# Reordering the first pass of an adaLN + ternary-FFN kernel: attended values next to scores, out products one unit later, ternary compares in halves

## What is computed

```python
# x (32, 32, 256), cond (32, 256); 16 heads of 128
ada = cond @ ada_w + ada_b                       # shift1, scale1, gate1, shift2, scale2, gate2
x1 = _ln(x) * (1.0 + scale1) + shift1
q, k, v = x1 @ qkv_w + qkv_b                     # reshaped (32, 32, 3, 16, 128)
attn = softmax(einsum('bthd,bshd->bhts', q, k) * scale)
x = x + gate1 * (einsum('bhts,bshd->bthd', attn, v) @ out_w + out_b)
x2 = _ln(x) * (1.0 + scale2) + shift2
x = x + gate2 * (gelu(x2 @ ffn_w1 + ffn_b1) @ ffn_w2 + ffn_b2)
# then x + bitffn(x): three linear layers whose weights are made ternary,
# wq = round(tanh(w / mean|w|)) * arctanh(mean|w|), and whose inputs are quantised to 8 bits
```

## Time and profile before

| what | value |
|---|---|
| median of three runs | 317.27 us (315.52, 317.27, 318.60) |
| profiled execution, its own time | 314.79 us |
| its span in the profile | 313.0 us |
| between the two | 1.79 us |
| TensorE busy, share of the span | 305.9 us, 98% |
| granted TensorE clock, mean | 1.00 |

### The profile page before, as it was taken

One profiled execution on the slowest core, in us unless ns is written; L12 is line 12 of the kernel. 1 busy time (PEld: TensorE's weight loads), 2 busy tenths in 40 slices (PEclk: granted clock), 3 DMA queues, 4 the chain that ended last, 5 costly groups with the idle time before them and its releaser, 6 DMA issues.

```text
span 313.0 us, 9827 instructions
## 1 busy us (share of the span) xinstructions
PE 305.9 (98%) x4171; PEld 271.4 (87%) x4171; DVE 223.7 (71%) x451; ACT 185.7 (59%) x358; POOL 128.0 (41%) x109
## 2 busy tenths in 40 slices
PE   8999999999999999999999999999999999999986
PEld 6888989899898989989898998789997789998664
DVE  3675889847795994634569057879277888996996
ACT  2765474645534664466344936587655677468793
POOL 2366406200930992766120621147330255323590
PEclk9999999999999999999999999999999999999999
DMA  7789944500044546210020010200010200200011
GB/s 234 268 227 274 290 148 181 168 4 2 2 116 89 162 114 235 69 36 2 3 70 2 2 35 3 63 7 2 20 50 2 69 4 2 69 0 2 0 36 68
DMA packets 21171, 24.49 MB, mean 78 GB/s; under 512 B 2020, under 2 KB 18696, under 8 KB 21128
## 3 DMA queue, kind: packets, MB, share of 16 engines
q1 hardware_dynamic: 20752, 23.57, 25.0%
q10 hardware_dynamic: 376, 0.30, 0.3%
HBM read 22.74 MB, written 1.11 MB: 76 GB/s over the span
## 4 chain that ended last, share of the span: by engine, by line
PE 93%; DVE 2%; ACT 2%; issue 1%; ACTq 0%; DVEq 0%
PE proj_banks L589 43%; PE out_bank L589 16%; PE wide_banks L589 5%; PE turn_bank L589 5%; PE proj_banks L654 4%; PE att_banks L685 4%; PE wide_banks L884 2%; PE att_banks L589 2%; PE wide_banks L685 2%; PE att_banks L931 2%; PE att_banks L918 1%; ACT work L1977 1%; PE wide_banks L768 1%; PE att_banks L884 1%; PE proj_banks L884 1%
## 5 line engine op out<-in xcount | busy, mean ns | idle before, releaser
L1834 ACT ACTIVATE q_t<-proj_banks,bias_cols 128x256 f32<-128x256 f32 x64 | 30.4, 475 | 48.6 <-PE proj_banks L589 47.8
L589 PE MATMUL proj_banks<-x_hi,w_hi 128*128 128x256 f32 x252 | 52.5, 290 | 0.0
L589 PE MATMUL proj_banks<-x_hi,w_lo 128*128 128x256 f32 x252 | 49.6, 278 | 0.0
L589 PE MATMUL proj_banks<-x_lo,w_hi 128*128 128x256 f32 x252 | 49.6, 278 | 0.0
L589 PEld LDWEIGHTS proj_banks<-x_hi,w_hi 128*128 128x128 f32 x252 | 38.6, 188 | 3.6 <-issue 1.6
L589 PEld LDWEIGHTS proj_banks<-x_hi,w_lo 128*128 128x128 f32 x252 | 38.3, 188 | 0.0
L589 PEld LDWEIGHTS proj_banks<-x_lo,w_hi 128*128 128x128 f32 x252 | 38.2, 188 | 0.0
L1305 DVE TENSOR_TENSOR v_sb<-proj_banks,bv_row 128x512 f32<-128x512 f32 x32 | 22.0, 687 | 17.1 <-PE proj_banks L589 15.9
L1834 ACT ACTIVATE k_t<-proj_banks,bias_cols 128x256 f32<-128x256 f32 x64 | 30.1, 470 | 0.0
L1839 ACT ACTIVATE scores<-scores 128x256 f32<-128x256 f32 x16 | 6.7, 418 | 32.2 <-DVE scores L1314 32.2
L1337 DVE STREAM_TRANSPOSE att_banks<-att_banks 128x512 f32<-128x512 f32 x16 | 11.6, 727 | 18.4 <-PE wide_banks L685 17.9
(11 more groups left out here) (329 smaller groups left out, 790.5 us busy)
## 6 DMA issues: line engine op xcount, KB each, us to landing
stage<-in_L_cond_qkv_w SPq DMA_DIRECT2D x16, 256.0 KB, 3.6
gate<-gate_rows_scratch SPq DMA_DIRECT2D x48, 64.0 KB, 2.5
stage<-in_L_cond_qkv_w SPq DMA_DIRECT2D x4, 512.0 KB, 5.1
stage<-in_L_cond_out_w SPq DMA_DIRECT2D x16, 128.0 KB, 4.3
work<-in_L_ffn_w SPq DMA_DIRECT2D x2, 1024.0 KB, 5.6
xin<-in_x SPq DMA_DIRECT2D x7, 256.0 KB, 2.9
bv_row<-in_L_cond_qkv_b SPq DMA_DIRECT2D x4, 256.0 KB, 6.4
work<-in_L_cond_ada_w SPq DMA_DIRECT2D x1, 1024.0 KB, 8.7
```

Source lines behind the costliest of these rows:

```text
L589: mm = pe.matmul(dst, l, r, start=start and i == 0, stop=stop and i == len(seq) - 1)
L1834: act.activation(dst[:, h, :], proj_bank[h % 2][:, s * QT:(s + 1) * QT], ACT.Identity, bias=bias_cols[:, c:c + 1]).then_inc(qk_kept, 1)
```

## The change

1. In units 2 to 7 (`V_LAST`) TensorE runs head 0, 1, 2, 3, then attend(u - 1), score(u), v 0, v 1. To make room, heads, scores and value rows swap the halves of `proj_banks` from unit to unit (`head_bank`, `packed(u)`, `v_bank`). The second value unit now waits for `shifted` (the scores have been read), score(u) no longer for a value row.
2. Out products of u - 1 move into unit u + 1, behind its head 1 (those of 0 stay in unit 1).
3. `tern_turn` moves to units 5, 7 and 9; each pair of compares is split (`tern_below`, `tern_make`) over two units. The third pair is now in unit 8, its transposes follow score(9), and its two copies (`tern_keep(2, 0)` and `(2, 1)`) stand on ScalarE ahead of heads 0 and 1 of unit 10.
4. On VectorE `softmax_shift(u)` moves between the two `at_turn`; on ScalarE `exponent(u)` between the two `at_high`, and `acc_keep` ahead of head 2 of units 3, 5 and 7.
5. On SyncE the wait for `tern_turned` at 6 and the load of g3 move behind later loads. `split_qk(2, 0)` on VectorE moves ahead of the tail of unit 6.

```diff
-    TERN_UNITS = (3, 5, 6)
+    TERN_UNITS = (5, 7, HALF + 1)
+    V_LAST = range(2, HALF)
...
-        packed = proj_bank[0][:, 0:2 * HG * TB]
+        def head_bank(u, h):
+            return proj_bank[(h + u) % 2 if u in V_LAST else h % 2]
+        def packed(u):
+            return head_bank(u, 0)[:, 0:2 * HG * TB]
+        def v_bank(u, t):
+            return head_bank(u, 1 - t if u in V_LAST else t)
...
             sp.dma_start(f2_stage, ffn2_d).then_inc(f2_in, 16)
-            sp.wait_ge(tern_turned, 2 * len(TERN_ORDER))
-            sp.dma_start(g3_row[:, :], row(g3)).then_inc(g3_in, 16)
             sp.wait_ge(v_kept, 2 * HALF)
             load_bv(3)
             wo_split(2)
             load_wo(3)
             sp.wait_ge(gate1_read, 4)
             load_gate(gate1, 0, 0, gate1_in)
+            sp.wait_ge(tern_turned, 2 * len(TERN_ORDER))
+            sp.dma_start(g3_row[:, :], row(g3)).then_inc(g3_in, 16)
...
+                elif h == 0 and u - 1 in V_LAST:
+                    pe.wait_ge(v_kept, 2 * u - 1)
...
-                pe.wait_ge(qk_kept, 2 * HG * u + 2 * HG - 2 + 2 * t)
+                if u in V_LAST and t == 1:
+                    pe.wait_ge(shifted, u + 1)
+                else:
+                    pe.wait_ge(qk_kept, 2 * HG * (u + 1) - (0 if u in V_LAST else 2 - 2 * t))
...
-                elif u in TERN_UNITS:
-                    pe.wait_ge(tern_kept, 2 * TERN_UNITS.index(u) + 2)
+                elif u + 1 in TERN_UNITS[:2]:
+                    pe.wait_ge(tern_kept, 2 * TERN_UNITS.index(u + 1) + 2)
+                elif u == TERN_UNITS[2]:
+                    pe.wait_ge(tern_kept, 2 * len(TERN_UNITS))
...
+                if u in TERN_UNITS:
+                    tern_turn(TERN_UNITS.index(u))
+                if u > 2:
+                    for t in range(2):
+                        out_proj(u - 2, t)
                 qk_unit(u, 2)
-                if u > 1:
+                qk_unit(u, HG - 1)
+                if u in V_LAST:
                     attend(u - 1)
-                qk_unit(u, HG - 1)
+                    score(u)
...
                 v_unit(u, 0)
                 v_unit(u, 1)
                 score(u)
+                if u in TERN_UNITS:
+                    tern_turn(TERN_UNITS.index(u))
                 out_proj(u - 1, 0)
...
             def attention_tail(u):
+                at_turn(u - 1, 0)
+                if u in V_LAST:
+                    softmax_shift(u)
+                at_turn(u - 1, 1)
+                keep_v(u, 0)
+                at_low(u - 1, 0)
+                if u in V_LAST:
+                    keep_v(u, 1)
+                at_low(u - 1, 1)
...
             softmax_norm(HALF - 1)
+            below = tern_below(2, n)
...
+                if q == 0:
+                    tern_make(2, below)
...
                 for h in ((1, 0, 2, 3) if u == 1 else range(HG)):
-                    if u - 1 in TERN_UNITS and h < 2:
-                        tern_keep(TERN_UNITS.index(u - 1), h)
+                    if h == 2 and u in TERN_UNITS:
+                        for b in range(2):
+                            tern_keep(TERN_UNITS.index(u), b)
+                    if h == 2 and u > 2 and u % 2 == 1:
+                        acc_keep(u // 2 - 1)
                     keep_qk(u, h)
...
                 for h in range(HG):
+                    if u - 1 == TERN_UNITS[2] and h < 2:
+                        tern_keep(2, h)
                     keep_qk(u, h)
```

More of the change, by code:

```diff
@@ L647, in score @@
                 pe.wait_ge(qk_kept, 2 * HG * (u + 1))
-                pe.wait_ge(v_kept, 2 * u + 1)
+                if u not in V_LAST:
+                    pe.wait_ge(v_kept, 2 * u + 1)
                 for t in range(2):
@@ L653, in score @@
                             tok = slice(t * P + j * TB, t * P + (j + 1) * TB)
-                            mm = pe.matmul(packed[j * TB:(j + 1) * TB, cols], q_t[:, h, tok], k_t[:, h, tok],
+                            mm = pe.matmul(packed(u)[j * TB:(j + 1) * TB, cols], q_t[:, h, tok], k_t[:, h, tok],
                                            start=True, stop=True)
@@ L762, in tern_turn @@
                     pe.wait_ge(tern_kept, 2 * p)
-                pe.wait_ge(at_lo_made, 2 * TERN_UNITS[p])
+                pe.wait_ge(at_lo_made, 2 * TERN_UNITS[p] - (2 if TERN_UNITS[p] in V_LAST else 0))
                 for b in range(2):
@@ L1282, in tern_make @@
                     dve.wait_ge(tern_turned, 2 * (p - 1))
-                n = own.up(dve.tensor_scalar(dst, tern_stage[i], thr[:, i, 1:2], None, ALU.is_lt))
+                return own.up(dve.tensor_scalar(dst, tern_stage[i], thr[:, i, 1:2], None, ALU.is_lt))
+            def tern_make(p, n):
+                i, dst = TERN_ORDER[p], tern[p % 2]
                 after(n)
@@ L1603, in _ @@
                         late_conditions()
+                    else:
+                        tern_make(0, below)
                     x1_make(u // 2 + 1)
@@ L1606, in _ @@
                     x_norm(3)
-                    tern_make(0, tern_thresholds(0))
+                    below = tern_below(0, tern_thresholds(0))
                 elif u == 5:
-                    tern_make(1, tern_thresholds(1))
+                    below = tern_below(1, tern_thresholds(1))
                 elif u == 6:
-                    tern_make(2, n)
+                    tern_make(1, below)
+                    split_qk(2, 0)
                 elif u == 7:
@@ L1615, in _ @@
                     split_qk(3, 0)
-                attention_tail(u)
+                if u > 0:
+                    attention_tail(u)
                 if u == 5:
@@ L2009, in _ @@
                 if u > 0:
-                    for t in range(2):
-                        at_high(u - 1, t)
+                    at_high(u - 1, 0)
+                    if u in V_LAST:
+                        exponent(u)
+                    at_high(u - 1, 1)
                 if u == 0:
@@ L2029, in _ @@
                     load_table(ACT.Exp)
[L2030 to L2035, removed]
             for q in range(NQ):
```

39 lines of the change are left out of this document (18 added, 21 removed).

## The result

| | before | changed |
|---|---|---|
| median, the two run by turns (22 executions each) | 315.44 us | 318.07 us |
| ratio of the times, 95% interval | | 1.0065 [1.0043, 1.0088] |
| profiled execution: span | 313.0 us | 316.1 us |
| mean granted clock in it | 1.00 | 0.995 |

A forecast was written before the change was run, and what follows sets the result against it. TensorE's issue of matmuls was taken as the bound. First pass -1.2 + 0.2 + 0.4 = -0.6 us, plus 2.6 us waiting for g3, made +2.0 on 317.27: 319.3 us, 0.6% slower, range 316.2 to 322.2.

The forecast's parts named there:

- Edit 1: Units 2 to 7: attend and score side by side remove 0.20 us of tile-shape losses in each, -1.2 us.
- Wait (a): Score(u) on TensorE, 1.00 us behind head 3, needs ScalarE's copy of it; 0.03 a unit, 0.2 us in all.
- Wait (b): Value unit 1 on TensorE waits for VectorE's shift of the scores; slack 0.4 us, nothing charged.
- rival C: Units 4 to 7: at_turn on VectorE over 0.4 us late, delaying value unit 1; 2 us more, chance 0.12.
- Edit 2: Out products moved later, between two runs of 256 columns on TensorE: no shape change or wait, nothing charged.
- Edit 3: Ternary transposes in units 5 and 7, between head 1 and out products: loss on both sides, 0.4 us.
- The row of gains: Attend(9) in unit 10 waits for ScalarE's work queued behind the later load of g3; 2.6 us.
- L: Time the load of g3 takes to land after SyncE issues it; taken as 4.4 us, ends 3.4 and 7.7.
- L - 1.8: TensorE's wait before attend(9): the landing time of g3 less 1.8 us; 2.6 us, ends 1.6 and 5.9.
- the estimate of 4.8: Landing of g3 by a fixed 2 us plus growth with bytes: 4.8 us, making attend(9)'s wait 3.0 us.
- Rival D: The clock falls in the new wait before attend(9), slowing it and two heads; up to 3.9 us more, chance 0.04.

The follow-up runs named there:

- shape_between: copies_first with one full-array matmul of 128 columns, its result unread, between attend and score in units 6 and 7; one execution, 313.84 us.
- copies_first: The changed kernel with both ternary copies of unit 10 ahead of the scaling of g3 on ScalarE; 314.27 us, ratio to before 0.9972.
- scale_late: The changed kernel with only the scaling of g3 moved behind exponent(10) on ScalarE; 314.91 us, ratio to before 0.9997.
- row_twice: The changed kernel with g3 loaded twice, one load behind the other, ScalarE waiting for both; 322.72 us, ratio to before 1.0231.
- scale_between: The changed kernel with the scaling of g3 between head 0's copy and the second ternary copy on ScalarE; 315.20 us, ratio to before 1.0013.

## Why the prediction was right

The sign, the place and the size held, +2.05 us against +2.0; the absolute time was 1.2 us too high: the kernel before took 315.44 beside the changed one, 1.8 less than the 317.27 of the three runs shown before, and the medians lie 0.6 further apart than forecast. Point by point:

- **Edit 1, -1.2 us: right.** Nothing is lost between the 32x32 and the 128x32 shape, and shape_between measures 0.19 for the 0.20 a unit. The Trainium skill, page TensorEngine Tiling (Array Packing), section Key Properties, has every change of mode drain TensorE; by that reading 0.5 us would have been left, and the trace does not bear it out: attend costs 1.00 us in front of score as in front of a head.
- **Wait (a), +0.2: too much.** In the changed kernel's profile score starts 1.00 us behind attend and head 3's copy isn't felt; in copies_first's it cost 0.15 us once, in unit 2.
- **Wait (b) and rival C: right that nothing is charged, wrong in the count.** VectorE was to be just in time in unit 7. It idled 3.20 us before at_turn there:

```profile
105.24 0.69 DVE L1291 CAST w_hi<-stage 128x1024 fp32r<-128x1024 f32 x1
106.88 0.70 DVE L1285 CAST w_hi<-stage 128x1024 fp32r<-128x1024 f32 x1 [0.95 <-DMA stage<-in_L_cond_qkv_w]
...
110.78 0.73 DVE L1365 STREAM_TRANSPOSE att_banks<-att_banks 128x512 f32<-128x512 f32 x1 [3.20 <-PE wide_banks L701]
```

  The same roundings took 1.78 in rows 7. I had carried over durations that hold only in their old company. GpSimd's timeline here, where `accumulate` comes later with the out products (edit 2):

```profile
107.71 1.29 POOL L2263 TENSOR_TENSOR xa<-xa,out_b_row 128x512 f32<-128x512 f32 x1 [3.03 <-ACT xa L1886]
```

  It is idle while both roundings run; in the kernel before it worked from 104.45 to 114.00 with no pause over 0.1 us, beside both of 1.78. The kernel before shows the same within itself: its L1260 rounds 128x1024 in 0.68 us at 100.67, with GpSimd idle, and in 1.71 at 102.66, beside a subtraction of GpSimd that runs from 101.43 to 103.82. That the one makes the other fits all four, but no run changed GpSimd's work alone. The smallest slack of all units is 0.59 us, in unit 2, where I had seen no danger.
- **Edit 2, nothing:** no wait appears in its place. Neither it nor edits 4 and 5 were tried alone.
- **Edit 3, +0.4: too much.** TensorE in unit 7, out products behind the transposes:

```profile
102.97 1.07 PE L784 MATMUL wide_banks<-ident_h,tern_odd 128*128 128x128 f16 x16
103.84 0.72 PE L597 MATMUL out_bank<-wo_hi,at_hi 128*128 128x256 f32 x4
104.39 0.64 PE L597 MATMUL out_bank<-wo_lo,at_hi 128*128 128x256 f32 x4
```

  The 16 cost 0.87, as before, and the four behind them 0.55 for 0.47. That is one loss of 0.08 more a unit, not two. With wait (a) at nothing the sum is -1.2 + 0.2 = -1.0, and -1.05 was read from the two profiles, with the scatter said above.
- **The row of gains, 2.6: mechanism right, L mis-sized.** L was 3.75, not 4.4. The formula L - 1.8 gives 1.95, and 2.08 came. Plain weights of the same size were the nearest row (3.9 in rows 13), nearer than the doubling of bytes that made me go up. But the same load in the same place took 3.4 (scale_late), 3.5, 3.7 to 4.0 (row_twice), 3.9, 4.1, 4.3 twice and 4.8 us (shape_between) in the other profiles, so the 4.4 lies inside the scatter of landings: by how much one profile misses it is in part luck, and so is the nearness of 1.95 to 2.08. The Trainium skill, page DMA: Bandwidth & Descriptors, section Anatomy of one DMA — SWDGE (gpsimd) path, gives its fixed 2 us for a DMA that GpSimd issues. This one is issued by SyncE, so the estimate of 4.8 carries the figure over to another path. 4.8 is the longest landing of the nine profiles.
- **Rival D: it happened, where I gave it 0.04.** Its price of "up to 3.9" was too high, 1.27, since the low level lasted 3.4 us and the matmuls near its ends lost little. My reason against it was that no wait of this length stood in the trace. That is no reason: a profile without long waits says nothing on what one would cost. Counted at every second execution it adds 0.6 us, and -1.05 + 2.08 + 0.6 = 1.6 is inside the measured [1.4, 2.8]. It filled the space that two terms, each overestimated, had left, so +2.0 owes part of its precision to errors that cancel.

## What to carry to other kernels

When a load is moved, don't stop at the engine that waits for it: add up what stands behind that wait on the same engine, and compare the end with the due time of whoever reads that. Here 0.75 us of idle time on ScalarE was 2.08 on TensorE. The cure is order, not speed: what the bound engine waits for goes ahead of what merely has to be done, and the change then is worth the 1 us that it was to give. And a new wait on TensorE is priced twice, by its length and by the clock behind it: here 1.3 us on top of a wait of 2.0, in half of the executions.

## What the runs showed of the hardware that I had not expected

- **A clock that falls in some executions only.** With 2.0 us without a matmul 10 of 20 executions had the lower mean clock, with 1.5 us none of 10, with 5.8 us all of the 4. Yet the 1.37 us in row_twice's opening brought the lower level, where 1.51 (scale_between) and 1.28 (scale_late, ahead of score(1)) left it at 1.00 in their profiles: the length of the wait alone doesn't decide, and what else does is open. The Trainium skill, page TensorE: Matmul & The Clock Gate, section What's actually happening, has the clock follow what TensorE did just before; the trace agrees, with a fall that in the changed kernel comes only as TensorE starts anew.
- **Two spacings for one matmul.** Matmuls of 256 columns follow one another at 0.113 us in some stretches and 0.118 in others, both at the full clock. In unit 6 of the changed kernel pairs start 0.23 apart (94.13, 94.36, 94.58, 94.81) and in unit 7 nearer 0.235 (108.16, 108.40, 108.63, 108.87). Which one holds changes at a break and from run to run. It moves a first pass by some 0.5 us: scale_late's, without a wait of TensorE in it, took 112.84 for 112.30. I found no cause.
- **An opening that scatters.** The condition rows start between 33.01 and 34.81 us in nine profiles with the same opening, and at 35.84 in row_twice's, which has a wait of 1.4 us and a lowered clock ahead of them. Two spans alone could not have shown a change of 1 us in the first pass; the table by parts comes nearer, to about half a microsecond.
